# Attention stage: order of TensorE's work within a block, a contiguous row for the key bonus, and a scan moved ahead

## What is computed

```
x = layernorm(x)
Q = normalize(x @ W_q.T), K = normalize(x @ W_k.T)      # 16 heads of 4
V = x @ W_v.T                                           # 16 heads of 64
Qn = normalize(Q @ W_nudge)
scores = Qn @ K.T * 0.5 + k_bonus[key]                  # k_bonus from sigmoids of K @ simple_roots.T
attn = softmax(causal mask of scores)
x = x + layernorm((attn @ V) @ W_out.T)
```

## Time and profile before

| what | value |
|---|---|
| median of 3 runs | 1754.74 us |
| profiled execution | 1755.85 us |
| its span in the trace | 1754.1 us |
| attention rounds | about the first 750 us of it |
| PE / DVE / ACT / POOL busy over the span | 94% / 75% / 51% / 57% |
| the same from 171 to 217 us (two rounds) | PE 45.65, DVE 38.56, ACT 30.21, POOL 37.57 of 46 us |

### The profile page before, as it was taken

The page is one execution under the profiler, slowest core; times in us unless marked ns, Lnnn a source line. Parts: engine busy times, 40 slices in busy tenths (PEclk is TensorE's granted clock), DMA queues, the critical chain, the costliest instruction groups (busy, mean ns, idle before and its releaser), DMA issues.

```text
span 1754.1 us, 47186 instructions
## 1 busy us (share of the span) xinstructions
PE 1642.4 (94%) x14905; PEld 1229.3 (70%) x14905; DVE 1317.4 (75%) x3869; ACT 888.7 (51%) x2003; POOL 1000.0 (57%) x1782
## 2 busy tenths in 40 slices
PE   4999999999999999959999999999999999989996
PEld 3677777777777777537778888878787887655553
DVE  5688888888888888645567777777777775858886
ACT  3666666666666666514444444444444443224443
POOL 7888888888888888712233333333333334227777
PEclk8999999999999999869999999999999999999998
DMA  1011111111111113010120000000000001634441
GB/s 43 11 57 55 54 54 49 51 47 47 49 54 54 54 54 105 14 37 16 52 78 22 29 26 29 31 26 29 26 29 30 30 25 49 209 127 130 138 128 41
DMA packets 78259, 95.96 MB, mean 55 GB/s; under 512 B 7046, under 2 KB 62995, under 8 KB 78160
## 3 DMA queue, kind: packets, MB, share of 16 engines
q1 hardware_dynamic: 70992, 77.91, 14.1%
q0 software_dynamic: 7168, 16.87, 2.7%
HBM read 53.14 MB, written 43.69 MB: 55 GB/s over the span
## 4 chain that ended last, share of the span: by engine, by line
PE 40%; DVE 8%; issue 4%; POOL 2%; ACT 1%; DMA 0%; DVEq 0%; POOLq 0%; SPq 0%; ACTq 0%
PE main L1371 6%; PE main L1373 5%; PE main L1380 5%; PE main L1536 3%; PE yp L1451 3%; PE xi L1286 2%; PE main L1311 2%; PE main L1435 2%; PE main L1324 2%; PE main L1438 1%; PE main L1436 1%; PE route L1550 1%; PE xi L1550 1%; POOL out L1269 1%; PE turn L1279 1%
## 5 line engine op out<-in xcount | busy, mean ns | idle before, releaser
L662 ACT ACTIVATE wgu<-score 128x384 f32<-128x384 f32 x512 | 223.2, 490 | 80.8 <-PE score L484 79.4
L1371 PE MATMUL main<-hT_high,h_high 128*128 128x512 f32 x512 | 221.2, 432 | 0.9 <-ACT hT_high L1636 0.9
L1373 PE MATMUL main<-hT_high,h_low 128*128 128x512 f32 x512 | 201.3, 393 | 0.0
L506 PE MATMUL outp<-wgu 128*32 128x256 f32 (+1 forms) x4096 | 196.1, 333 | 1.9 <-POOL wgu L327 0.8
L327 POOL TENSOR_SCALAR_AFFINE_SELECT wgu<-wgu 128x512 f32<-128x512 f32 x256 | 165.8, 653 | 50.0 <-ACT wgu L662 32.6
L506 PEld LDWEIGHTS outp<-wgu 128*32 128x32 f32 x4096 | 116.4, 111 | 68.2 <-issue 23.5
L1380 PE MATMUL main<-hT_low,h_high 128*128 128x512 f32 x512 | 138.2, 391 | 0.1
L1944 DVE SCALAR_TENSOR_TENSOR th<-th,main 128x512 f32<-128x512 f32 x64 | 43.9, 685 | 114.5 <-ACT th L1663 114.5
L544 PE MATMUL back<-wout,wgu 128*128 128x128 f32 x1024 | 128.5, 280 | 0.0
L544 PEld LDWEIGHTS back<-wout,wgu 128*128 128x128 f32 x1024 | 121.7, 195 | 0.4
L1269 POOL DMA_INDIRECT out<-res,idx x96 | 96.5, 1005 | 44.4 <-issue 40.9
(11 more groups left out here) (301 smaller groups left out, 4351.4 us busy)
## 6 DMA issues: line engine op xcount, KB each, us to landing
sorted_d<-row_buf SPq DMA_DIRECT2D x26, 772.0 KB, 3.7
xg<-sorted_d SPq DMA_DIRECT2D x48, 386.0 KB
wgu<-in_gate_up SPq DMA_DIRECT2D x4, 2048.0 KB, 8.8
xa<-in_x SPq DMA_DIRECT2D x32, 128.0 KB, 3.5
xr<-in_x SPq DMA_DIRECT2D x32, 128.0 KB, 3.2
x_d<-x SPq DMA_DIRECT2D x32, 128.0 KB, 1.9
x1c<-x_d SPq DMA_DIRECT2D x16, 256.0 KB, 2.7
x1v<-x_d SPq DMA_DIRECT2D x16, 256.0 KB, 2.7
```

What stands on the lines that cost most here:

```text
L506: m = pe.matmul(outp[AUG * j:AUG * (j + 1), p % 2, k * P:T], val[par][:, k, h, v:v + AUG], weights(h, k), start=(k == 0), stop=(k == 1), t ...
L662: act.activation(prob[:, h // 2 % (RING // 2), :, h % 2, :], score[h % BANKS][:, 0:SC].rearrange("p (c q) -> p c q", q=P), ACT.Exp).then_i ...
L1371: pe.matmul(main[m % 2][:, :], w[0][:, k, m * P:(m + 1) * P], src[0][:, k, :], start=(k == 0), stop=False)
L1373: pe.matmul(main[m % 2][:, :], w[1][:, k, m * P:(m + 1) * P], src[0][:, k, :], start=False, stop=False)
```

## The change

It has six parts, all in the attention.

1. `weighted` no longer waits for both pairs' masks at its start; it waits for each pair's own mask ahead of that pair's products.
2. On TensorE the q/k product stands behind `scores(b, par, 2)` instead of ahead of it, and on ACT its squares stand behind the exponentials of heads 4 and 5.
3. The third quarter of the values stands behind `scores(b, par, 5)` instead of ahead of `scores(b, par, 4)`, on ACT its copy behind the exponentials of heads 10 and 11.
4. Behind that, TensorE's order is: values 2, spread 1, `cmax` transpose, values 3, `qkn` transpose, spread 2, key transposes, rotation product. Before it was: spread 1, `qkn` transpose, values 3, `cmax` transpose, spread 2, rotation product, key transposes.
5. DVE copies `bonT` and scans it ahead of `scaled`.
6. The bonus goes to a new tile `bonus_row`, one float after another, and L607's transposes read that; one more POOL instruction copies it into the fifth column of `k5`, with a semaphore of its own (`bon_k`), for which the splitting of the keys waits. `late_constants` clears the new tile once.

```diff
         def weighted(b, par, g):
-                wait(pe, s["masked"], PAIRS_A * b + 2 * g + 2)
                 ...
                 for p in (2 * g, 2 * g + 1):
+                    wait(pe, s["masked"], PAIRS_A * b + p + 1)
                     for k in range(2):
         # tensor step
                 values(f, par, 0)
+                scores(b, par, 2)
                 if n is not None:
                     ...
                         mm = pe.matmul(front[:, T + i * P:T + (i + 1) * P], xnT[par][:, i * P:(i + 1) * P], wqk[:],
                     mm.then_inc(s["p_qk"], 1)
-                scores(b, par, 2)
                 weighted(b, par, 0)
                 ...
-                        mm = pe.matmul(turned[:, i * P:(i + 1) * P], k5_wide[:, i * HEADS:i * HEADS + P, DH], ident[:],
+                        mm = pe.matmul(turned[:, i * P:(i + 1) * P], bonus_row[:, i * HEADS:i * HEADS + P], ident[:],
                 ...
-                values(f, par, 2)
                 ...
+                values(f, par, 2)
                 spread_out(z, 1)
         # vector step
                 normalise(z, par, 0)
-                scaled(n)
                 if f is not None:
                     wait(dve, s["p_bonT"], f + 1)
                     ...
+                scaled(n)
                 normalise(z, par, 1)
         # gpsimd, bonus
                     out = bv[r][:].rearrange("p i h c -> p (i h) c") if r < 3 \
-                        else k5_wide[:, 0:TT * HEADS, DH:DH + 1]
+                        else bonus_row[:, 0:TT * HEADS].rearrange("p (r o) -> p r o", o=1)
                     did(pool.tensor_tensor(out, t, pair[:, :, :, 0], ALU.add))
+                    if r == 3:
+                        pool.tensor_scalar(k5_wide[:, 0:TT * HEADS, DH], bonus_row[:, 0:TT * HEADS], 1.0, 0.0,
+                                           ALU.mult, ALU.add).then_inc(s["bon_k"], 1)
```

More of the change, by code:

```diff
@@ L158, in attention_layer @@
         bonT = sb("bonT", [HEADS, T])
+        bonus_row = sb("bonus_row", [P, P + HEADS])
         cmax = sb("cmax", [P, T])
@@ L196, in attention_layer @@
                  "ssg1", "roots", "qkn", "p_qkT", "qkT", "p_rot", "sq2", "ek", "qraw", "ss2", "ssg2", "ek1",
-                 "sg", "q4", "kcopy", "bon", "p_bonT", "bonT", "cmax", "p_cmax", "q5", "ksplit", "qsplit", "kaug",
+                 "sg", "q4", "kcopy", "bon", "bon_k", "p_bonT", "bonT", "cmax", "p_cmax", "q5", "ksplit", "qsplit", "kaug",
                  "qaug", "p_kaT", "p_qaT", "kaT", "qaT", "p_v", "val", "p_score", "prob", "masked", "p_out", "raw",
@@ L206, in attention_layer @@
         N_IDENT = 4
-        N_CONST = 22
+        N_CONST = 23
         ctx.callback(clear, nc, list(s.values()))
@@ L295, in late_constants @@
                 const(pool.memset(k5_wide[:], 0.0))
+                const(pool.memset(bonus_row[:], 0.0))
                 const(pool.memset(cmax[:], 0.0))
@@ L420, in step @@
                     wait_apart(pool, s["kcopy"], f + 1, s["const"])
+                    wait_apart(pool, s["bon_k"], f + 1, s["const"])
                     wait_apart(pool, s["p_kaT"], f, s["const"])
@@ L614, in step @@
                 scores(b, par, 5)
+                values(f, par, 2)
                 spread_out(z, 1)
+                if f is not None:
+                    wait(pe, s["cmax"], f + 1)
+                    for i in range(TT):
+                        mm = pe.matmul(turned[:, T + i * HEADS:T + (i + 1) * HEADS], cmax[:, i * P:(i + 1) * P],
+                                       ident[:, 0:HEADS], start=True, stop=True)
+                    mm.then_inc(s["p_cmax"], 1)
+                values(f, par, 3)
                 if n is not None:
@@ L622, in step @@
                     mm.then_inc(s["p_qkT"], 1)
-                values(f, par, 3)
+                spread_out(z, 2)
                 if f is not None:
[L625 to L630, removed]
+                    wait(pe, s["q5"], f + 1)
+                    turn_operands(k_aug, "k", f)
                 if n is not None:
@@ L636, in step @@
                     mm.then_inc(s["p_rot"], 1)
-                if f is not None:
-                    wait(pe, s["q5"], f + 1)
-                    turn_operands(k_aug, "k", f)
                 scores(b, par, 6)
@@ L692, in step @@
                 copy_values(f, par, 0)
+                weights(b, 4, 5)
                 if n is not None:
@@ L697, in step @@
                                    ACT.Square).then_inc(s["sq1"], 1)
-                weights(b, 4, 5)
                 if n is not None:
@@ L705, in step @@
                 copy_values(f, par, 1)
-                copy_values(f, par, 2)
                 weights(b, 8, 9)
@@ L710, in step @@
                 weights(b, 10, 11)
+                copy_values(f, par, 2)
                 if n is not None:
```

## The result

| | kernel before | changed kernel |
|---|---|---|
| median (runs) | 1757.78 us (9: 1751.74 to 1760.22) | 1763.40 us (9: 1761.33 to 1765.37) |
| ratio, 95% interval | 1 | 1.0041 (1.0030 to 1.0053) |
| profiled execution / its span | 1755.85 / 1754.1 us | 1762.01 / 1760.0 us |
| last input transpose starts | 684.2 us | 692.3 us |
| mean round, rounds 5 to 30 (b = 3 to 28) | 22.305 us | 22.582 us |

The change makes the kernel 0.4% slower: 7.2 us by the ratio, against 9.0 us forecast, and a time of 1764 us.

A forecast was written before the change was run, and what follows sets the result against it. A loop of softmax sums, DVE's reciprocal, roots and scan, then TensorE's cmax transpose and what follows, bounds the rounds. 15 x (22.47 - 22.28) + 15 x (22.75 - 22.34) = 9.0 us slower gives 1764 us, range 1748 to 1777.

The forecast's parts named there:

- the forecast's 0.46: TensorE's bonus transposes and three products behind them: 1.36 us would become 0.90 with contiguous weights.
- 0.38: TensorE's q/k product behind scores 2: waiting and unhidden loads of 0.44 removed, less 0.06 for changes between products.
- the change of shape: TensorE going between scores, q/k product and weighted sums: net cost 0 to 0.10 us, taken as 0.06.
- The new wait: TensorE's cmax transpose: reached at 180.54 in A, starts at 181.27 behind DVE's scan, so TensorE stands for 0.7 us.
- The scan's end: DVE's scan in paired alternating rounds A and B: 0.33 us earlier by part 5, in A 0.13 later from masks.
- The rule that each mask delays DVE until its end: POOL's masks hold the SBUF ports shared with DVE for a whole instruction, so each delays DVE, however they lie.
- The 4 us more: By the port rule POOL's new copy would add its own 0.2 to both rounds, about 4 us on the sum.
- Behind the wait: TensorE from cmax transpose to next input transpose: 11.21 before, plus 0.70 and 0.22 moved, plus 0.17 loads: 12.30 us.
- The sum: Attention rounds b = 1 to 30, 15 of each kind: 2.9 + 6.2 = 9.0 us slower.
- No change: Rival: same loop, but B's scan comes as early as A's; both rounds 22.34, 1756 us; chance 0.19.
- Slower still: Rival: scan 0.4 us later in both rounds, or q5 ends too late for TensorE's key transposes; 1778 us, chance 0.18.
- Faster: Rival: the scan isn't what TensorE waits for, its own queue decides; 24 us less, 1731 us; chance 0.13 with between cases.

The follow-up runs named there:

- strided_bonus_read: Changed kernel with part 6 undone: bonus transposes again read the fifth column of k5, five floats apart; ratio 1.0037 to the kernel before.
- parts_1_2_6: Kernel before with only parts 1, 2 and 6, TensorE's old middle order and scaled ahead of the scan; ratio 1.0015 to the kernel before.
- changed_again: The changed kernel itself, unchanged, run on the chip of three later kernels; ratio 1.0040 to the kernel before.
- values_first_q5_early: Changed kernel with values 2 in its old place, values 3 ahead of the cmax transpose, spread 2 last, normalise 1 behind q5, ACT copies matching; ratio 0.9995.

## Why the prediction was right, point by point

**Part 6.** 192 ns a load instead of 316, and the bonus transposes take 178.85 - 178.31 = 0.54 to the scores, the assumed 0.44 and 0.10. strided_bonus_read takes 0.99 there, so 0.45 is saved. The working behind the forecast's 0.46 was unsound all the same: it took 0.23 for each of the two value products behind line 607, where the first of three takes 0.31 to 0.34 in every place, and in the old order, with the values behind, parts_1_2_6 shows 0.18.

**Part 2.** From the values' last product to the weighted sums, with scores and q/k product between: 174.92 - 173.68 = 1.24. Before it was 1.48: from 171.97 to the scores at 173.18, and from scores to weighted sums 0.27 (174.01 to 174.28, the same step into another product). So 0.24 is saved, not 0.38. The mis-sized term is the change of shape: the product between scores and weighted sums takes 0.64 (174.28 to 174.92), 0.20 more than the bare 0.44. It lies ahead of the wait and so cost the forecast nothing. TensorE is free for the `cmax` transpose 9.58 us into A (182.28 + 0.23 - 172.93), where the forecast had 9.31.

**The new wait.** Forecast: transpose 0.05 behind a scan that ends 0.33 earlier, TensorE standing about 0.7 us. Measured: 0.05, and 0.55 to 0.70.

**The scan's end**, after the input transpose: A 10.12 forecast, 10.08 measured; B 10.40 forecast, 10.23 measured. In A the gap between the masks closed as forecast (one row of 1.31 for both, against 0.66, a gap of 0.24 and 0.66), but that put the scan's start back by 0.04 and not 0.13, and the scan itself took 1.01 instead of 0.96. In B the exponentials came earlier and the masks take 1.24 instead of 1.40, so DVE is free 0.15 sooner; the prediction had left that out. The rule that each mask delays DVE until its end holds for line 773 (0.57 for 0.26), but the new copy added nothing: line 772, which started 0.06 behind it, took its usual 0.26 and ended 0.07 behind the copy. The Trainium skill (SBUF — State Buffer, section "SBUF: two separate sides") has VectorE and GpSimd share one pair of SBUF ports as a lock held for a whole instruction; the trace agrees for the masks. The 4 us more that the prediction worked out from it took the whole 0.2 of the copy as lost to DVE, and didn't come.

**Behind the wait**: 12.30 forecast; 195.45 - 183.06 = 12.39 and 218.12 - 205.73 = 12.39 measured. Three sizes were off. The `cmax` transpose takes 0.46 to the next product instead of 0.36, so the loads that nothing hides cost 0.10 and not 0.17; the fourth quarter of the values takes 0.79 (183.52 to 184.31) and not 0.70; and the key transposes with the rotation product take 1.07 (184.74 to 185.81) where they took 0.99 before (182.88 to 183.87).

**The sum.** A +0.24 (forecast 0.19), B +0.33 (forecast 0.41). In rounds 5 to 30, 26 rounds x 0.277 = 7.2 us. The rounds at b = 1 and 2, the first two of the forecast's 30, went from 22.34 to 22.89, 0.55 each and not 0.3, which adds 1.1 us. The last input transpose starts 8.1 us later and the last product with W_out 7.0 us later (773.26 against 766.22): behind the rounds the changed kernel gains 1.1 us. The rest of the program took 986.8 us instead of 987.9, which makes 5.9 us in the span; that difference says nothing, since the same rest took 988.0 in changed_again and 986.6 to 992.7 in the traces of the other kernels.

So the mechanism was right. That the time came out at 1763.40 against 1764 is luck in part: the kernel before had a median of 1757.78 in the nine runs, 3.0 us above the 1754.74 that the forecast started from, and the change cost 7.2 us by the ratio instead of 9.0. Within a round errors cancel too: in B the scan's end came 0.17 early and what stands behind it was 0.09 longer.

**The rivals.** No change needed a scan 0.41 earlier in B than forecast (22.75 - 22.34); it was 0.17 earlier. Slower still needed a scan end at 10.5 or later; it was 10.23 at most. Faster needed TensorE's queue to decide. Its price, 24 us, was wrong besides: values_first_q5_early shows a round in which the wait for the scan is gone, and it takes 22.21, not 21.5. Of the 0.7 between, 0.28 is part 6, which saves 0.18 there (0.61 + 0.90 against 0.81 + 0.88) instead of 0.46, and 0.15 is part 2. The rest, 0.3, lies between the sixth and the seventh scores: the `qkn` transposes take 0.46 to the next product instead of 0.22 in the changed kernel, since the loads of the key transposes wait 0.28 for `q5`. That kernel has an order of its own, so it gives the price of TensorE's queue only roughly.

## What to carry to other kernels

An engine that is 94% busy can still be in a loop with another one: look for the place where it takes something back from a chain that it started itself, and note the distance between the chain's end and its reader (here 0.75 and 0.40 us). A move that puts the reader earlier, or more work behind it, is paid in full as soon as that distance is used up, and every saving ahead of it is worth next to nothing, until the chain gets shorter or other work stands between it and its reader, as in values_first_q5_early. Undoing such parts one at a time says little: of six parts here, two change almost nothing when they are undone, and one pair works only together. Once TensorE ran ahead, a 0.25 us copy on POOL, the third engine, cost 0.10 us a round; without it the kernel has a ratio of 0.9982, which its rounds don't explain.

## What the runs showed of the hardware

- A load of 128 fp32 weights from addresses 20 bytes apart takes 316 ns, from contiguous ones 192 ns, and the four passes behind them 0.54 us to the scores instead of 0.99 (the changed kernel and strided_bonus_read), but 0.61 instead of 0.81 where value products follow (parts_1_2_6 and the kernel before).
- A DVE step of 0.26 us that starts under a POOL mask ends about 0.1 us after it: 0.57, and in longer waits 0.61 to 0.74. The scan behaves alike: it takes 0.74 us when POOL's instruction under way ends 0.13 us into it, 0.91 when it ends 0.37 into it (204.62 + 0.52 against 204.77) and 1.01 when it ends 0.47 into it. In both longer cases 0.53 to 0.54 is left behind the end of POOL's instruction. So it is the moment of the start that counts, not whether POOL is at work.
- Four full-array passes between row-tiled scores and column-tiled sums take 0.64 us, elsewhere 0.44: some 0.1 for each change of shape, if that is the cause; no run takes the shapes apart.
- TensorE's idle times of up to 0.9 us a round didn't change the granted clock, which stands at 1.00 of full speed, 2.4 GHz, from 171 to 401 us in all 14 traces.
